# A top-p graph kernel: values below the threshold in a tile of their own, and step one's pass units divided four, one, one and two

## The reference, cut to what matters

```python
def _top_p_attention(X, W1, W2, W3):
    q = X @ W1.T @ W2.T
    k = X @ W3.T
    probs = softmax(q @ k.T)
    # keep, in each row, the largest values until their sum passes 0.9
    A = probs * mask
    return A / max(A.sum(-1, keepdims=True), 1e-12)

R = (S + eye(N)) / rowsum(S + eye(N))
Z = 0
Xf, Xa = X, X
for n in range(2):                      # step one, step two
    A = _top_p_attention(Xa, W1, W2, W3)
    Xf = R @ Xf
    Xa = A @ Xa
    Z = Z + Xf @ U1[n].T + Xa @ U2[n].T
h = X + Z                               # and a layer norm with gain and bias
```

## Time and profile before

| | us |
|---|---|
| median of three runs | 1009.66 |
| lowest and highest | 1006.43 and 1011.87 |
| the profiled execution | 1009.86 |
| its span, first to last instruction | 1008.1 |
| busy in the span: PE, DVE, ACT | 800.5, 664.4, 474.4 |

### The profile page before, as it was taken

One profiled execution on the slowest core, in us unless ns is written; L12 is line 12 of the kernel. 1 busy time (PEld: TensorE's weight loads), 2 busy tenths in 40 slices (PEclk: granted clock), 3 DMA queues, 4 the chain that ended last, 5 costly groups with the idle time before them and its releaser, 6 DMA issues.

```text
span 1008.1 us, 11952 instructions
## 1 busy us (share of the span) xinstructions
PE 800.5 (79%) x3886; PEld 547.4 (54%) x3886; DVE 664.4 (66%) x2092; ACT 474.4 (47%) x945; POOL 69.2 (7%) x63
## 2 busy tenths in 40 slices
PE   4879984988888837568698688785698899994894
PEld 4844432756666726465375566565295485552342
DVE  5967868488597788832879878768777212235715
ACT  4886334336556483224535846856945141024111
POOL 0020001010000000000000000100001200013001
PEclk9889986988989977879697898989799999997898
DMA  9849502544004000000063400601342719200001
GB/s 332 333 167 429 212 10 84 170 164 136 33 1 168 1 1 2 0 2 1 2 213 120 167 1 1 225 2 53 135 167 85 283 52 413 86 1 0 1 0 42
DMA packets 20219, 108.23 MB, mean 107 GB/s; under 512 B 1824, under 2 KB 8752, under 8 KB 9776
## 3 DMA queue, kind: packets, MB, share of 16 engines
q1 hardware_dynamic: 18752, 106.77, 28.5%
q10 hardware_dynamic: 1392, 0.61, 0.2%
HBM read 88.23 MB, written 19.14 MB: 107 GB/s over the span
## 4 chain that ended last, share of the span: by engine, by line
PE 52%; DVE 22%; ACT 13%; issue 8%; POOL 2%; DMA 2%; DVEq 1%; POOLq 0%; SPq 0%; ACTq 0%
PE PS L795 11%; PE PS L600 6%; PE PS L664 6%; PE PS L534 6%; PE PS L717 5%; DVE AT L1513 4%; PE PS L864 4%; DVE mxv L1652 3%; DVE nd L1516 3%; ACT BC L1236 3%; PE PS L1045 3%; PE PS L1021 3%; ACT AT L1236 3%; DVE AT L2122 2%; PE PS L1051 2%
## 5 line engine op out<-in xcount | busy, mean ns | idle before, releaser
L1067 ACT ACTIVATE AT<-PS 128x512 f32<-128x512 f32 (+2 forms) x240 | 118.7, 560 | 132.6 <-PE PS L534 100.4
L534 PE MATMUL PS<-ident,AT 128*128 128x128 f32 x544 | 84.4, 290 | 47.9 <-DVE rS L2178 21.7
L1652 DVE TENSOR_REDUCE mxv<-PS 128x1 f32<-128x2048 f32 x32 | 73.2, 2288 | 68.7 <-PE PS L717 68.4
L717 PE MATMUL PS<-K,ST 64*128 64x512 f32 x256 | 87.0, 770 | 14.6 <-ACT EA L1204 7.8
L534 PEld LDWEIGHTS PS<-ident,AT 128*128 128x128 f32 x544 | 67.8, 150 | 56.3 <-DVE rS L2178 24.5
L2122 DVE MAX8 AT<-AT 128x8 f32<-128x256 f32 (+2 forms) x336 | 92.4, 347 | 0.7
L795 PE MATMUL PS<-hr,AT 128*128 128x128 f32 x512 | 71.7, 290 | 7.7 <-ACT AT L1067 6.9
L795 PE MATMUL PS<-AT 128*128 128x128 f32 x512 | 70.4, 286 | 7.9 <-ACT AT L1067 7.3
L795 PEld LDWEIGHTS PS<-hr,AT 128*128 128x128 f32 x512 | 65.4, 200 | 15.8 <-ACT AT L1067 10.5
L795 PEld LDWEIGHTS PS<-AT 128*128 128x128 f32 x512 | 64.1, 197 | 16.9 <-ACT AT L1067 10.9
L1067 ACT ACTIVATE ST<-PS 128x512 f32<-128x512 f32 (+3 forms) x43 | 23.9, 562 | 103.5 <-PE PS L1051 23.8
(11 more groups left out here) (297 smaller groups left out, 1369.4 us busy)
## 6 DMA issues: line engine op xcount, KB each, us to landing
AT<-keep_at SPq DMA_DIRECT2D x32, 1024.0 KB, 5.1
EA<-in_adj SPq DMA_DIRECT2D x20, 1024.0 KB, 6.6
keep_at<-AT SPq DMA_DIRECT2D x8, 2048.0 KB, 25.0
AT<-keep_at SPq DMA_DIRECT2D x8, 2048.0 KB, 12.4
AT<-in_adj SPq DMA_DIRECT2D x12, 1024.0 KB, 6.2
EA<-keep_degrees SPq DMA_DIRECT2D x1, 1024.0 KB, 6.6
keep_x<-K SPq DMA_DIRECT2D x4, 256.0 KB, 6.9
out<-EA SPq DMA_DIRECT2D x4, 256.0 KB, 2.3
```

Of the source, the lines that this page charges most:

```text
L534: return pe.transpose(dst, src, ident[0:p, 0:p])
L717: return pe.matmul(bank(to + n), ST[1][half_rows, k * P:(k + 1) * P], keys[half_rows, n * BK:(n + 1) * BK], start=True, stop=True)
L1067: return act.activation(dst, src, ACT.Copy)
L1652: v(dve.tensor_reduce(mxv[:, odd:odd + 1], PS[:, b:b + 4, :], AX.XY, ALU.max))
```

## The change

1. `under` writes into `scratch`, AT's row 10, for all four tiles in turn, and no longer into `cands[k]`. The wait for `e_turned` goes from `under` to each mask (in a step's last group, one wait for all tiles ahead of the masks). Since the four tiles now share one scratch, a wait for the own MAX8 instructions stands behind each tile's. Row 10's second list tile moves to row 9 (`top_tile`).
2. In the groups outside `BOTH`, the row maxima of the next group's tiles 1, 2 and 3 stand behind the first `under` and half way through the MAX8 of tiles 1 and 2, instead of one and one ahead of the first `under` and one behind the second. `guess_gap` and `guess_first` of the next group go from the third tile's MAX8 into the first and third of the rounds.
3. `logit_mean(gi + 2)` goes, in every group that has it, from behind the rounds to behind `load_more`, just ahead of the masks.
4. `UNITS_IN` is (4, 1, 1, 2, 6, 2, 0, 0) in place of (6, 2, 0, 0, 6, 2, 0, 0). Units of step one's last group wait for its last queries, and one of ACT's sums goes ahead of the unit's copies. `third_sum`, which no group called, is gone.

```diff
-UNITS_IN = (6, 2, 0, 0, 6, 2, 0, 0)
+UNITS_IN = (4, 1, 1, 2, 6, 2, 0, 0)
...
+        scratch = row[:, 10, :]
...
                 for k in range(G):
-                    if gi > 0:
-
-                        dve.wait_ge(e_turned, 4 * (G * (gi - 1) + k + 1))
+                    under(v, scratch, E, q.th, k, accum_out=Lw[:, k:k + 1])
                     if gi not in BOTH and k == 0:
-                        next_max(2)
-                    under(v, E, q.th, k, accum_out=Lw[:, k:k + 1])
+                        next_max(1)
                     v.wait()
-                    if gi not in BOTH and k == 1:
-                        next_max(3)
...
+                        if s == sets // 2 and k in (1, 2) and gi not in BOTH:
+                            next_max(k + 1)
...
+                    v.wait()
...
-                if left > 1:
-                    logit_mean(gi + 2)
                 crossing_checked(q)
                 doubtful()
...
                 load_more()
+                if left > 1:
+                    logit_mean(gi + 2)
                 if left > 0:
-                    masked(v, E)
+                    for k in range(G):
+                        if gi > 0:
+
+                            dve.wait_ge(e_turned, 4 * (G * (gi - 1) + k + 1))
+                        mask_tile(v, E, k)
+                else:
+
+                    dve.wait_ge(e_turned, 4 * G * gi)
...
                         elif step == 0:
-                            sums_below(step, g + 1, 0, (0, 1))
+                            sums_below(step, g + 1, 0, (0, 1, 2))
                             unit_next()
-                            sums_below(step, g + 1, 0, (2, 3))
+                            sums_below(step, g + 1, 0, (3,))
```

More of the change, by code:

```diff
@@ L146, in gnn_kernel, with top_tile @@
         unit_st = [row[:, 8, 2 * BK + q * UNIT:2 * BK + (q + 1) * UNIT] for q in range(2)]
-        tops_at = [(row[:, 9, 0:BK], row[:, 10, 3 * BK:4 * BK]), (row[:, 9, BK:2 * BK], row[:, 9, 2 * BK:3 * BK])]
-        tops_of = [[half_[:, 0:sets * G * TOP].rearrange("p (k e) -> p k e", k=G) for half_ in pair]
-                   for pair, sets in zip(tops_at, SETS)]
+        scratch = row[:, 10, :]
+        tops_of = [[row[:, 9, m * BK:m * BK + SETS[step] * G * TOP].rearrange("p (k e) -> p k e", k=G)
+                    for m in ((0,), (1, 2))[step]] for step in range(STEPS)]
+        def top_tile(step, m, k):
+            if m == 0 or step == 1:
+                return tops_of[step][m][:, k, :]
+            at = (1 + k // 2) * BK + k % 2 * SETS[0] * TOP
+            return row[:, 9, at:at + SETS[0] * TOP]
         set_ends = [[(m * N + sets // 2) // sets for m in range(sets + 1)] for sets in SETS]
@@ L689, in queries @@
                     pe.wait_ge(z_ok, G * (gi - 1 if gi == NB + 1 else gi - 2))
[L690 removed]
+                issued = units_by(NB - 1 if gi == NB else NB * step + (1 if g == 3 else 0))
                 if g == 2:
@@ L739, in unit @@
                     pe.wait_ge(z_ok, G * (NB * step + g))
+                if step == 0 and g == NB - 1:
+                    pe.wait_ge(q_out, NB + 1)
                 unit_sums(u)
@@ L2055, in surely @@
                 for k in range(G):
-                    under(w, E, hi, k)
+                    under(w, cands[k], E, hi, k)
                 w.wait()
@@ L2119, in group @@
                             next_max(k + 2)
-                        if s == sets // 2 and k == 2 and left > 0:
+                        if s == sets // 2 and k in (1, 2) and gi not in BOTH:
+                            next_max(k + 1)
+                        if s == sets // 2 and k == 2 and gi in BOTH:
                             guess_gap(gi + 1)
-                        v.put(dve.max(tops[0][:, k, s * TOP:(s + 1) * TOP], cands[k][:, ends[s]:ends[s + 1]]))
-                    if k == 2 and left > 0:
+                        v.put(dve.max(top_tile(step, 0, k)[:, s * TOP:(s + 1) * TOP], scratch[:, ends[s]:ends[s + 1]]))
+                    if k == 2 and gi in BOTH:
                         guess_first(gi + 1)
                         dve.sem_inc(th_ok, 1)
-                v.wait()
-                v.put(total(seen8, tops[0][:, :, TOP - 1:sets * TOP:TOP], ALU.max))
+                    v.wait()
+                v.put(total(seen8, tops_of[step][0][:, :, TOP - 1:sets * TOP:TOP], ALU.max))
                 for m in range(WINDOW // TOP):
@@ L2131, in group @@
                         for k in range(G):
[L2132 to L2133 removed]
+                            v.put(dve.match_replace(top_tile(step, m % 2, k), L[:, k, (m - 1) * TOP:m * TOP],
+                                                    top_tile(step, (m - 1) % 2, k), 0.0))
                         v.wait()
                     for k in range(G):
[L2136 removed]
+                        v.put(dve.max(L[:, k, m * TOP:(m + 1) * TOP], top_tile(step, m % 2, k)))
                     v.wait()
[L2138 to L2139 removed]
+                    if gi not in BOTH and left > 0:
+                        if m == 0:
+                            guess_gap(gi + 1)
+                        if m == 2:
+                            guess_first(gi + 1)
+                            dve.sem_inc(th_ok, 1)
                 crossing_checked(q)
```

42 lines of the change are left out of this document (8 added, 34 removed).

## The result

| | us |
|---|---|
| before, median of four runs | 1009.26 (1006.43 to 1011.87) |
| changed, median of four runs | 1031.93 (1031.16 to 1032.62) |
| ratio, with its 95% interval | 1.0217 (1.0191 to 1.0243) |
| the changed kernel's profiled execution, its span | 1031.76, 1030.0 |

The change makes the kernel 2.2% slower: 22.7 us, where 21 were forecast.

A forecast was written before the change was run, and what follows sets the result against it. No engine was taken as the bound by itself; what counts is who is waited for at each hand-over among PE, DVE and ACT. 1009.86 - 10.0 (step one) + 15.6 + 15.5 (late means) = 1031.0 us, range 1023.5 to 1038.5.

The forecast's parts named there:

- The deciding step: Step two's first two groups: `logit_mean` comes late, PE's unit waits for it; 15.6 and 15.5 us lost, +31.1 in all.
- The clock term: Step two's late units: after idleness PE runs at the lower clock, 9.45 us from unit start to ACT's copy, not 7.66.
- Step one's sum: Step one: units moved later and DVE's shorter lists together gain 10.0 us, bounds 5 to 12.
- if DVE's lists gained nothing, the units alone would still give about 7: Step one: the new division of units would by itself give about 7 of the 10.0 us.
- DVE's kept values: Step one: they come near 372.5 for the third `attend` and near 420 for the fourth, so PE no longer waits.
- The moved lists cost no instruction: Whole kernel: moved lists, dropped helper and row 9 add no instruction; the new waits cost 0.3 us.
- the late mean is hidden and only step one is left: Rival, step two: the late mean costs nothing, step one's 10.0 us gain stays, 999.9 us; chance 0.07.
- Half of it: Rival, step two's second group: DVE some 8 us earlier, mean 8.6 us late and not 16.8; 1023 us, chance 0.08.
- Nothing from step one: Rival, step one: the two last units take 19.6 us where 16.88 us were idle, gain gone; 1041 us, chance 0.07.
- advice not to fit the clock ramp: Whole kernel: the skill puts the ramp under 1%; leaving out every clock term, the sum would be about 1029.

The follow-up runs named there:

- e1: Changed kernel with step two's `logit_mean(gi + 2)` back ahead of `crossing_checked` in both groups; 1005.08 us, ratio 0.9952 to before.
- e2: Changed kernel with `logit_mean` back ahead of `crossing_checked` in step two's first group alone, the second's still late; 1015.65 us.
- e3: Kernel before with only step two's `logit_mean(gi + 2)` moved behind `load_more`, just ahead of the masks; 1044.73 us, ratio 1.0326.
- e6: Changed kernel with step two's `logit_mean(gi + 2)` behind `doubtful`, ahead of the last tile's sum; 1007.45 us.
- e4: Kernel before with only step one's units divided 4, 1, 1, 2, their query wait and order of sums; 1010.67 us, ratio 1.0023.
- e5: Changed kernel's lists and row maxima alone, units 6, 2, 0, 0 and every `logit_mean` as in the kernel before; 1002.96 us, ratio 0.9917.
- e8: e5 with the row maximum of the next group's tile 1 ahead of the first `under` again in step two; 992.46 us, ratio 0.9841.
- e10: Changed kernel, late means kept, with the row maximum of tile 1 ahead of the first `under` in step two; 1031.32 us.

## Why the prediction was right, and where it was not

- **The deciding step held.** Both units start over 14 us after the logits ahead of them, released by `gs`, 29.7 us in all (29 forecast), and ACT idles 18.16 and 18.18 us ahead of its copies. The cause is shown by taking it away (e1, e2), by adding it alone (e3) and by a smaller dose (e6).
- **Its size was somewhat low.** 15.6 and 15.5 were forecast, 16.2 and 17.9 measured in the changed kernel, 16.1 and 17.2 in e3. The lateness was right, 14.5 and 14.6 us from the queries to the unit (14.6 and 14.8 forecast). The clock term was too small: from a unit's start to ACT's copy the forecast took 9.45 us, and it was 10.3 in both groups (557.89 to 568.21, 650.02 to 660.35). Net of where their queries start, the logits behind come 16.1 us late in the first (585.70 against 578.35, and 8.8 for the queries) and 16.4 in the second (679.84 against 656.03, less 7.4). Another 1.4 us of the second's 17.9 arise behind those logits; where was not traced.
- **Step one's sum held, its reasons did not.** Net of the first stretch the gains at the four `attend` are 3.2, 8.4, 8.8 and 8.6 us (2.8, 7.8, 10.3 and 8.0 forecast), and 11.2 (10.0) by the stretch of step one. But "if DVE's lists gained nothing, the units alone would still give about 7" is refuted: e4 gives nothing and e5 all of it. The step that failed is the price of the units alone, which left DVE out at the fourth `attend`. In e4 PE is 3.2, 4.3 and 3.5 us early at the first three, and then begins the fourth with DVE's first mask, which is 1.0 us early; on the way it waits 6.48 and 2.91 us for DVE. The prediction placed DVE's kept values for the changed kernel, at the third `attend` (near 372.5) and the fourth (near 420), and never for the units alone.
- **"The moved lists cost no instruction" was true and beside the point.** One `under` of 2.35 us in front of a row maximum costs 3.3 and 3.8 us in e1's two stretches and 6.7 and 3.7 in e5's (against e8). It did not spoil the number, because the late mean covers it (e10). A prediction for e1 by the same working would have said 999.9, and 1005.1 was measured: the rival "the late mean is hidden and only step one is left" had too good a price.
- **Nothing was forecast behind step two, and 3.4 us came** (241.1 to 237.7, below), and 3.2 us of bad luck with the clock ahead of the second queries went against it. These two cancel, and so in part do two more: step one's stretch and the one behind it came out 2.0 us better than forecast and the late means 3.0 us worse. That the total was less than 1 us off in the profiled execution (1031.0 and 1031.76) is luck; that it lay some 20 us above before is not.
- **The other rivals.** "Half of it" (the second mean 8.6 us late) fails at the wait of 15.17 us. "Nothing from step one" fails at the stretch of 254.6. The Trainium skill's advice not to fit the clock ramp ("TensorE: Matmul & The Clock Gate", What's actually happening) would have had 1029. The clock terms were there: net of the queries, the first late unit took 10.3 us to its copy where it took 7.66 before, the second 10.3 where it took 8.70. That is 4.3 us, 0.4% of the time and within the page's 1%, but an eighth of what the late means cost.

## What to carry to other kernels

A small instruction that another engine waits for must be placed by who waits, not by where it is convenient: past a long block it costs that block. Before a second stream is moved out of an engine's way, ask of each other engine how far behind it is at every later hand-over, since what that engine does not gain is waited out there. A loss can hide under a larger one: after the big one is found and removed, read the waits again, because what comes out from under it can be worth as much as the change was meant to give.

## What the runs showed of the hardware

**POOL is slower beside DVE's masks.** The rest of the kernel is shorter with the new lists in every trace: 236.8 to 238.6 us in ten, against 241.1 to 242.6 in the three with the old lists. POOL in the kernel before, then two of DVE's masks there, then POOL in the changed kernel:

```profile
781.55 2.07 POOL L469 TENSOR_SCALAR nd<-nd 128x4 f32<-128x4 f32 x1 [14.48 <-ACT hr L1289]
...
783.71 3.00 POOL L471 TENSOR_TENSOR es<-nd,ex 128x4 f32<-128x4 f32 x1
```

```profile
781.23 2.35 DVE L1513 SCALAR_TENSOR_TENSOR AT<-AT,s 128x2048 f32<-128x2048 f32 x1
...
783.50 2.35 DVE L1513 SCALAR_TENSOR_TENSOR AT<-AT,s 128x2048 f32<-128x2048 f32 x1
```

```profile
806.80 0.20 POOL L476 TENSOR_SCALAR nd<-nd 128x4 f32<-128x4 f32 x1 [14.49 <-ACT hr L1298]
...
807.20 1.01 POOL L478 TENSOR_TENSOR es<-nd,ex 128x4 f32<-128x4 f32 x1 [0.20 <-POOL nd L476]
```

The same two small instructions take 2.07 and 3.00 us beside the masks of step two's last group, and 0.20 and 1.01 once those are over. It is so in all thirteen traces: 1.94 to 2.16 and 3.00 us in the three with the old lists, 0.19 to 0.20 and 1.01 in the ten others. The first ends at 783.62, just behind a mask, the second at 786.71, 0.86 us behind the last one. ACT's next scaling waits for them (5.63 us, then 1.87), and PE for ACT (3.13 us before, none in the changed kernel). With the new lists the masks end before POOL comes. No run tried this alone, and the 1.7 us by which e1's rest is longer than e5's are not explained by it. The Trainium skill ("SBUF — State Buffer", Who interferes with whom) states that a VectorE instruction with two SBUF inputs and a GpSimd instruction that reads SBUF exclude each other, and that the later one stands until the other is done; the trace agrees.

**The same code meets different clocks.** The first stretch took 216.1 to 222.8 us in thirteen traces. e10 and the changed kernel have one and the same code in it and took 218.8 and 222.0, with the first unit begun at 0.70 and at 1.22 us for two matmuls. That row parts all thirteen: the six traces with 0.70 took 216.1 to 219.7 us, the seven with 1.22 took 220.6 to 222.8. The kernel before ran between 1000.8 and 1013.2 us in the twenty runs beside e1 to e4. What sets the state at that unit is not shown. The Trainium skill ("TensorE: Matmul & The Clock Gate", What's actually happening) says that the count of slow matmuls differs between runs of one kernel; these two traces agree. For differences of a few microseconds here, stretches of the trace told more than medians.
